# Gated linear attention: three item banks, transposed q and k, and what ScalarE copies

## The reference, cut to what matters

```python
q = _l2norm((h @ Wq).reshape(B, T, N_HEADS, D_K))
k = _l2norm((h @ Wk).reshape(B, T, N_HEADS, D_K))
v = (h @ Wv).reshape(B, T, N_HEADS, D_V)
alpha = jax.nn.sigmoid(h @ Wg).reshape(B, T, N_HEADS, D_K)
def step(S, inp):
    a_t, k_t, v_t, q_t = inp
    S = a_t[..., None] * S + k_t[..., None] * v_t[..., None, :]
    o_t = jnp.einsum('bhkv,bhk->bhv', S, q_t)
```

## Time and profile before

| | |
|---|---|
| runs, median (lowest to highest) | 3381.13 us (3378.74 to 3383.21) |
| profiled execution, and its span | 3380.03 us, 3378.2 us |
| busy share of the span | PE 70%, DVE 61%, ACT 37%, POOL 34% |
| mean granted TensorE clock | 0.826 |
| gated linear attention, sequences 0 to 14 | 94 to 905.5 us |
| its last sequence, to the next layer's first instructions | 905.5 to 956.9 us |

### The profile page before, as it was taken

One profiled execution on the slowest core, in us unless ns is written; L12 is line 12 of the kernel. 1 busy time (PEld: TensorE's weight loads), 2 busy tenths in 40 slices (PEclk: granted clock), 3 DMA queues, 4 the chain that ended last, 5 costly groups with the idle time before them and its releaser, 6 DMA issues. The chain is left out here.

```text
span 3378.2 us, 47699 instructions
## 1 busy us (share of the span) xinstructions
PE 2351.0 (70%) x15091; PEld 1611.0 (48%) x15091; DVE 2056.1 (61%) x5571; ACT 1244.7 (37%) x2671; POOL 1156.1 (34%) x1205
## 2 busy tenths in 40 slices
PE   2899999999955347624928988566998889740190
PEld 0566666666644225413705555454555555430070
DVE  3677777777744694530156665585888888645016
ACT  1333343434334102201304555226777777410030
POOL 2242423323200000144521110116777777511551
PEclk9999999999987557856958888677999999855595
DMA  7200000000010000002232223000000000000122
GB/s 222 65 1 0 0 0 0 0 0 0 0 57 0 0 0 0 0 28 57 61 93 73 69 72 106 0 0 1 1 0 0 0 0 0 0 0 11 53 59 77
DMA packets 105711, 93.62 MB, mean 28 GB/s; under 512 B 12252, under 2 KB 92150, under 8 KB 105462
## 3 DMA queue, kind: packets, MB, share of 16 engines
q1 hardware_dynamic: 97942, 76.72, 8.3%
q0 software_dynamic: 7680, 15.81, 1.4%
HBM read 62.02 MB, written 46.26 MB: 32 GB/s over the span
## 5 line engine op out<-in xcount | busy, mean ns | idle before, releaser
L2613 POOL TENSOR_SCALAR mb_w<-mb_duT,mb_bT 128x256 f32<-128x256 f32 x512 | 464.3, 930 | 143.8 <-PE bank L2623 138.1
L2549 DVE TENSOR_TENSOR_SCAN mb_hs<-mb_dA,bank 128x512 f32<-128x512 f32 x256 | 300.9, 1205 | 30.7 <-issue 24.5
L2642 PE MATMUL bank<-mb_hc,ident 128*128 128x512 f32 x512 | 250.4, 612 | 25.2 <-DVE mb_hc L2559 24.0
L634 POOL TENSOR_TENSOR e_w<-e_w,gla_az 128x2048 f32<-128x2048 f32 x16 | 72.4, 4523 | 485.8 <-ACT gla_az L394 485.8
L1893 DVE TENSOR_REDUCE ra_mx<-bank 128x2 f32<-128x512 f32 x256 | 167.1, 688 | 99.0 <-PE bank L1770 97.0
L2604 ACT ACTIVATE mb_dA<-mb_delta,mb_A 128x255 f32<-128x255 f32 x512 | 217.6, 494 | 3.6 <-DVE mb_hs L2549 3.4
L509 ACT ACTIVATE gla_sT<-bank 128x128 f32<-128x128 f32 x256 | 69.3, 277 | 325.6 <-DVE gla_sT L537 319.4
L1979 ACT ACTIVATE ra_pT<-bank 128x512 f32<-128x512 f32 x256 | 139.2, 595 | 130.2 <-PE bank L1790 129.2
L2623 PE MATMUL bank<-ident,mb_w 128*128 128x128 f32 x1024 | 149.1, 279 | 35.6 <-DVE mb_hs L2549 26.2
L1544 ACT ACTIVATE e_hid<-bank,e_b 128x512 f32<-128x512 f32 (+1 forms) x128 | 81.2, 634 | 235.2 <-PE bank L1563 232.3
L38 POOL TENSOR_TENSOR scrap<-ones 128x1 f32<-128x1 f32 x96 | 20.0, 208 | 407.2 <-DVE ra_qk L1887 260.4
(11 more groups left out here) (509 smaller groups left out, 6492.0 us busy)
## 6 DMA issues: line engine op xcount, KB each, us to landing
results<-const_empty SPq DMA_DIRECT2D x2, 4096.0 KB
e_got<-results SPq DMA_DIRECT2D x32, 256.0 KB, 3.3
rope_rows<-ra_part SPq DMA_DIRECT2D x48, 128.0 KB, 1.9
ra_k<-rope_rows SPq DMA_DIRECT2D x32, 192.0 KB, 3.2
ra_q<-rope_rows SPq DMA_DIRECT2D x32, 192.0 KB, 4.3
queue<-const_spare_rows SPq DMA_DIRECT2D x1, 4128.0 KB
e_x<-queue SPq DMA_DIRECT2D x8, 516.0 KB, 4.3
e_w<-in_L_ffn_w SPq DMA_DIRECT2D x2, 2048.0 KB, 8.0
```

The lines of the kernel that those rows point to most:

```text
L2549: dve.tensor_tensor_scan(hs[n // 2 % 2][:, n % 2, :, :].rearrange("p c t -> p (c t)"), dA[n % RD][:, :, :].rearrange("p c t -> p (c t)"), ...
L2613: ins = pool.tensor_scalar(w[n % RH][:, h, :], duT[k][:, h, :], bT[k][:, h, n:n + 1], None, ALU.mult)
L2642: ins = pe.matmul(YB[:, :], g.ident[:, :], hc[grp % 2][:, j, :, :].rearrange("p c t -> p (c t)"), start=(n == 0), stop=(n == NS - 1))
```

## The change

The token-by-token projections of k and q are kept: ScalarE copies each chunk to SBUF (`tok`) before it squares it, and the Square reads that copy. A bank is free after the copy. In `pe_project` the second projection of q and k goes, and the kept chunks are transposed instead, four transposes of 128x128, into a single bank `QK`. The bank that this frees is the third of `PREP`. `PLAN` moves q2 to step 4, q3 and v0 to step 5. The Ln stands behind k3 instead of k2. On GpSimd the k norms' power comes before the log gates. VectorE's masked copy takes the cross-tile block too, with ones in the mask there, and ScalarE's copy of it goes. The spread norms are copied by ScalarE.

```diff
-    c["seen"] = np.concatenate([seen, seen], 1).astype(np.int32)
+    c["seen"] = np.concatenate([seen, seen, np.ones((P, P))], 1).astype(np.int32)
...
-    QK, PREP, EX, SC, OB = (pb[0], pb[2]), (pb[1], pb[7]), pb[3], pb[4:6], pb[6]
+    QK, PREP, EX, SC, OB = pb[0], (pb[1], pb[2], pb[7]), pb[3], pb[4:6], pb[6]
...
+    tok = {kind: [sb(f"{kind}tok{k}", [P, 2, HEADS * DK]) for k in R] for kind in "qk"}
...
-            4: ("q0", "q1", "v0"), 5: ("q2", "q3", "v1"), 6: ("v2", "", "v3"), 7: ("", "", "r")}
+            4: ("q0", "q1", "q2"), 5: ("q3", "v0", "v1"), 6: ("v2", "", "v3"), 7: ("", "", "r")}
...
-        return PREP[ORDER.index(item) % 2]
+        return PREP[ORDER.index(item) % 3]
...
-        return {"h": (h_ready, s + 1), "z": (z_ready, s * 4 + (c + 1)), "k": (ksq_ready, s * 4 + (c + 1)),
-                "q": (qsq_ready, s * 4 + (c + 1)), "v": (v_ready, s * 4 + (c + 1))}[kind]
+        return {"h": (h_ready, s + 1), "z": (z_ready, s * 4 + (c + 1)), "k": (ktok_ready, s * 4 + (c + 1)),
+                "q": (qtok_ready, s * 4 + (c + 1)), "v": (v_ready, s * 4 + (c + 1))}[kind]
...
             act.wait_ge(psum, s * 4 + (c + 1))
+            part = chunk_out(tok[kind][k], c)
+            act.activation(part, PB[:, :], ACT.Copy).then_inc(copied[kind], 1)
             if c:
                 act.wait_ge(summed, s * 4 + c)
             elif kind == "q":
                 act.wait_ge(kss_ready, s * 4 + 4)
-            act.activation(sq[:, :], PB[:, :], ACT.Square).then_inc(done, 1)
-        if item == "k2":
+            act.wait_ge(copied[kind], s * 4 + (c + 1))
+            act.activation(sq[:, :], part, ACT.Square).then_inc(done, 1)
+        if item == "k3":
...
-        if hp >= 2 or not first(s):
-            pe.wait_ge(mid_ready, 2 * at(s, hp - 2))
-        bank = QK[hp % 2]
-        pe.matmul(bank[:, 0:256], g.Wq[:, ch], hT[k][:, :], start=True, stop=True)
-        pe.matmul(bank[:, 256:512], g.Wk[:, ch], hT[k][:, :], start=True, stop=True).then_inc(qk_psum, 1)
+        if hp >= 1 or not first(s):
+            pe.wait_ge(mid_ready, 2 * at(s, hp - 1))
+        bank = QK
+        if hp == 0:
+            pe.wait_ge(ktok_ready, s * 4 + 4)
+            pe.wait_ge(qtok_ready, s * 4 + 4)
+        for j, kind in enumerate("qk"):
+            for t in range(2):
+                ins = pe.transpose(bank[:, j * 256 + t * P:j * 256 + (t + 1) * P], tok[kind][k][:, t, ch],
+                                   g.ident[:, :])
+        ins.then_inc(qk_psum, 1)
...
-            pe.wait_ge(cr_ready, at(s, hp - 1))
...
-        pe.wait_ge(cr_ready, at(s, hp))
...
-    def act_cross(act, s, hp):
-        for hd in range(2):
-            act.wait_ge(sc_ready, 2 * at(s, hp) - 1 + hd)
-            ins = act.activation(sT[hp % 2][:, hd, 2 * P:3 * P], SC[hd][:, 2 * P:3 * P], ACT.Copy)
-        ins.then_inc(cr_ready, 1)
+    def act_spread(act, s, hp):
+        act.wait_ge(o_psum, at(s, hp))
+        act.activation(rb[:, :], OB[:, 256:512], ACT.Copy).then_inc(rb_ready, 1)
...
-            dve.copy_predicated(sT[b][:, hd, 0:2 * P], g.seen[:, :], SC[hd][:, 0:2 * P]).then_inc(sc_ready, 1)
+            dve.copy_predicated(sT[b][:, hd, :], g.seen[:, :], SC[hd][:, 0:3 * P]).then_inc(sc_ready, 1)
 
     def dve_scale(dve, s, hp):
-        dve.wait_ge(o_psum, at(s, hp))
-        dve.tensor_copy(rb[:, :], OB[:, 256:512]).then_inc(rb_ready, 1)
...
+                    scales(i * 2 + k, 1, rnk[:, :, :], kss_ready, kmax_ready, rnk_ready)
                     log_gates(i * 2 + k, k)
-                    scales(i * 2 + k)
+                    scales(i * 2 + k, 0, rnq[:, :, :], qss_ready, qmax_ready, rnq_ready)
+                    parts(i * 2 + k)
...
-                  whole(lambda e, s, k, hp: act_exponentials(e, s, hp), lambda e, s, k, hp: act_cross(e, s, hp),
-                        none, act_item), end_of(lambda e, s, k, hp: act_cross(e, s, hp), none, None))
+                  whole(lambda e, s, k, hp: act_exponentials(e, s, hp), none,
+                        lambda e, s, k, hp: act_spread(e, s, hp), act_item),
+                  end_of(none, lambda e, s, k, hp: act_spread(e, s, hp), None))
```

More of the change, by code:

```diff
@@ L285, in gla @@
     names = ["hn", "hp", "h", "zp", "zm", "z", "ze", "zl", "lna", "kp", "ksq", "kss", "kmax", "rnk", "qp", "qsq", "qss",
-             "qmax", "rnq", "vp", "v", "rp", "rqT", "qkp", "ep", "ex", "qkx", "mid", "sp", "sc", "cr", "op", "rb", "o", "yp",
+             "qmax", "rnq", "vp", "v", "rp", "rqT", "ktok", "qtok", "qkp", "ep", "ex", "qkx", "mid", "sp", "sc", "op", "rb", "o", "yp",
              "y"]
@@ L289, in gla @@
      kss_ready, kmax_ready, rnk_ready, q_psum, qsq_ready, qss_ready, qmax_ready, rnq_ready, v_psum, v_ready, r_psum,
-     rqT_ready, qk_psum, e_psum, ex_ready, qkx_ready, mid_ready, s_psum, sc_ready, cr_ready, o_psum, rb_ready, o_ready, y_psum,
+     rqT_ready, ktok_ready, qtok_ready, qk_psum, e_psum, ex_ready, qkx_ready, mid_ready, s_psum, sc_ready, o_psum, rb_ready, o_ready, y_psum,
      y_ready) = [sig(n) for n in names]
+    copied = {"k": ktok_ready, "q": qtok_ready}
     def first(s):
@@ L317, in bank_free @@
     def bank_free(s, item):
-        i = ORDER.index(item) - 2
+        i = ORDER.index(item) - 3
         if i >= 0 and ORDER[i] == "y" and no_result(s):
-            i -= 2
+            i -= 3
         if i < 0 or (isinstance(s, int) and s == NSEQ):
             last = len(ORDER) - 1
-            i, s = last - (last - ORDER.index(item)) % 2, s - 1
+            i, s = last - (last - ORDER.index(item)) % 3, s - 1
         before = ORDER[i]
@@ L337, in pe_item @@
         PB = bank_of(item)
-        if not (first(s) and ORDER.index(item) < 2):
+        if not (first(s) and ORDER.index(item) < 3):
             sem, value = bank_free(s, item)
@@ L515, in dve_factors @@
         dve.wait_ge(ex_ready, at(s, hp))
-        q, kk, e = halves(QK[b][:, 0:256]), halves(QK[b][:, 256:512]), ex[b]
+        q, kk, e = halves(QK[:, 0:256]), halves(QK[:, 256:512]), ex[b]
         def factor(t, col, n):
@@ L634, in log_gates, with scales, parts @@
                 pool.tensor_tensor(lna[k], lna[k], az[:, :, :], ALU.subtract).then_inc(lna_ready, 1)
[L636 to L644, removed]
+            def scales(s, j, out, summed, bounded, done):
+                wait_apart(pool, g, summed, s * 4 + 4)
+                pool.tensor_scalar(ss[:, j, :, :], ss[:, j, :, :], 1e-24, None, ALU.max).then_inc(bounded, 1)
+                pool.wait_ge(bounded, s + 1)
+                pool.tensor_tensor(out, ss[:, j, :, :], halves(g.neg_half[:, 0:2 * HEADS]), ALU.pow).then_inc(done, 1)
+            def parts(s):
                 pool.wait_ge(rnq_ready, s + 1)
```

## The result

The changed kernel takes 3296.75 us (median; 3294.52 to 3297.76), the kernel before 3382.17 on the same chip: ratio 0.9743, interval 0.9729 to 0.9758, or 85 us less. Forecast were 105 less, 3275.5, range 3252 to 3342. The direction and the place were right, a fifth of the gain is missing. The profiled execution took 3296.06 us, span 3294.0.

The account below looks back on a forecast made before the run. TensorE was taken to bound the stage: 53.3 - 4.0 - 3.4 = 45.9 us, plus 1.4 and 0.35 of waits, 47.7 a sequence. Fifteen save 96 us, the last 3, the start 5.5: 104.5 less, 3275.5 us, range 3252 to 3342.

Parts of the forecast that it names:

- the gap in step 5: In the kernel before, q2 waits 2.06 us for q1's Square, then q3 1.58 us for v0's VectorE multiply.
- two kinds of sequences: Single sequences of the kernel before: 53.3 us at clock 1.00, or 54.8 to 55.4 us at 0.94, eight of fifteen slow.
- Transposes: Per-head q and k: four transposes instead of four matmul instructions, 0.86 us to 0.43 a step, 3.4 us a sequence saved.
- Three banks and Copies: Projection banks freed by a Copy, plus a third bank: 4.0 us of TensorE waits a sequence go.
- The sum: TensorE's issue of 45.9 us a sequence plus waits of 1.4 and 0.35 us around step 5: 47.7 us.
- ScalarE has about 1 us of cover: The spread norms, now copied by ScalarE, stand behind factors and mask in VectorE's order, so the scaling has that cover.
- rival A: The forecast itself: 3275 us, own range 3262 to 3292; chance 0.55.
- rival C: Steps 4 to 7: q chunks wait for banks again in pieces of 0.35 us, 2.5 us a sequence, 3313 us; chance 0.13.
- Rival F: Transposes let the clock fall to 1.2 GHz in light steps 7 and 0: 6.4 us a sequence, 3372 us; chance 0.03.
- The collision: Step 4's VectorE products get held by GpSimd's log gates, +4.8 us a sequence, 3347 us; forecast margin 0.1 us; chance 0.17.
- rival E: The collision plus a clock drop in every sequence: 55.5 us each, 3393 us; decides past 6.4 us a sequence; chance 0.04.
- Mask and copies: VectorE's masked copy grows to 570 ns, cross copies leave ScalarE, spread copies join it: 0.25 us latency against 0.26, nothing.

Follow-up runs that it names:

- e6: The changed kernel with per-head q and k projected again by matmul, into the same single bank, instead of transposed: 3328.18 us, ratio 0.9834.
- e9: The changed kernel with the log gates ahead of the k norms in GpSimd's list again, the Ln still behind k3: 3335.93 us, ratio 0.9858.
- e1: The changed kernel with the output projection y one item later in step 2, behind z3: 3271.08 us, ratio 0.9678.
- e4: The changed kernel with one memset of 512 columns on VectorE ahead of step 4's products, once a sequence: 3401.8 us, ratio 1.0068.
- e8: The changed kernel with the cross-tile block copied by ScalarE, the mask over 256 columns and the spread norms copied by VectorE: 3308.37 us, ratio 0.9779.
- e7: The changed kernel with two item banks and two banks for the transposes, as before the change: 3309.26 us, ratio 0.9778.

## Why the prediction was right, and what it missed

*What bounds the stage.* TensorE's issue time and the gap in step 5: right. e6 shows the first (3.42 us on TensorE a sequence), the changed kernel's waits the second. The reading of two kinds of sequences was too simple. Those of 54.8 to 55.4 us had 0.94 in six cases and 0.97 in two; of those of 53.3 to 53.5 us only two had 1.00, the other four 0.97:

```profile
363.80:417.17 53.37, 50.83 (x402) 34.68 (x397) 39.62 (x114) 20.94 (x49) 17.82 (x12) 0.97 0.00 0
```

Here TensorE is busy 1.4 us longer than at 1.00 and the sequence is as long, since its waits are 2.5 us instead of 3.8.

*Transposes.* 0.43 forecast, 0.44 measured. The row with the same count and shape was the one to go by; the pair alone would have said that nothing is gained.

*Three banks and Copies.* The 4.0 us of waits on banks went. The wait that the forecast put in their place before step 5 is 1.40 us as worked out, the scores' 0.51 against 0.35. Both came from walking through the written order of three engines with the durations of the trace of before. That the k norms come earlier was not needed: e9 has them late and no wait for v comes back.

*The sum.* Here is the step that failed: 45.9 + 1.4 + 0.35 a sequence left out y. The walk covered steps 4 to 7, up to the r item; steps 1 and 2 were not walked, but taken as hidden like the light steps. There VectorE has three z chunks at 1.3 us each beside products, masks and scaling, 6.9 us in a step that shrank to 6.1, and y, first in step 2, needs the scaling of that step. 1.42 us x 14 = 20 us, the difference between 3296.75 and 3275.5 nearly whole; e1 shows it. "ScalarE has about 1 us of cover" failed in the same place: VectorE idles 0.97 us for the spread copy.

The time lies 5 us outside rival A's own range (3262 to 3292), and the sequences of 49.1 us outside the 47 to 48.5 that were named as its sign. It is within the stated range by the room left for rival C, whose mechanism didn't occur: no chunk waits for a bank. That part is luck.

*The clock.* 1.00 behind the first sequence, as assumed. Two waits of 1.4 us in each sequence left it there. Rival F falls: 32 more transposes a sequence (four in each of eight steps), 1.00 granted. The Trainium skill's page "TensorE: Matmul & The Clock Gate", part 4, says that transposes don't count as busy in the same way. In a mix where they are 0.44 us of a light step of 3.2 nothing of it is seen.

*The collision.* The margin was not quite the forecast's: the products end 0.1 us after the log gates begin, not before, and pass because the last one starts first, by 0.11 to 0.18 us in every sequence. So the argument that both shift together is borne out. The rival's chance of 0.17 was no exaggeration: e4 shows what stood behind it. Its own price, 4.8 us, was right for the waits and left out the clock, which rival E had. E's turning point of 6.4 us a sequence leaves out the 8.5 us of start and end; with them it is 7.0. The first product of step 5 lost 0.17 us under the log gates, forecast 0.4, and it is hidden. The lock's rule of the page "SBUF — State Buffer" (the Trainium skill), section "Who interferes with whom", agrees with 4.59, 1.99 and 1.51 us of products under the log gates, and not with the power, during which products take 0.28.

*Mask and copies.* Forecast at nothing; e8 says 11.6 us together. VectorE's time was right (576 ns), but the cross copy on ScalarE delays the copy of the transposed tokens behind it, which a sum of latencies on one chain doesn't show.

*Start and end.* 5.5 and 3 us forecast, 6.7 and 4.6 measured.

Left open: why the unchanged later layers differ by up to 14 us between executions.

## What to carry to other kernels

In a static order across engines, walk the whole period, the steps with the most VectorE work above all, not only the step with the known gap: the next bound stands where an item that needs old results comes first in its step. Long instructions with table loads belong right behind the last thing that is urgent, and the long GpSimd instruction between two groups of VectorE instructions with two SBUF inputs; look at the margin in the trace before adding anything ahead of them. And count the clock with each wait: two waits of 1.4 us a sequence cost themselves; with one of 2.1 us (e7) ten sequences of fourteen lost 1.0 us more to the clock, with one of 2.2 (e9) six lost 1.5 to 3.0, and with one of 4.8 (e4) TensorE's busy time rose by 2.0 to 2.9.

## What the runs showed of the hardware

A VectorE product with two SBUF inputs that starts 0.09 us behind a 4.5 us GpSimd subtraction takes 4.59 us; one that starts 0.17 us ahead of it, and overlaps it by 0.11, takes 0.28, as does the same product beside GpSimd's 5.46 us power. TensorE's granted clock stayed at 1.00 with waits of 1.40 and 1.42 us in each sequence. With one of 2.08 beside one of 1.43 (e7) it was 0.97 in ten sequences of fourteen and 1.00 in four; with one of 2.21 (e9) 1.00 in eight, 0.97 in four and 0.94 in two; with one of 4.80 (e4) 0.94 in thirteen and 0.97 in one.
